# Stacked probability tails for attention, and slot normalisation on other engines, in an attention and soft-MoE kernel

## The reference

```
q = layernorm(x) @ Wq + bq;  k = ctx @ Wk + bk;  v = ctx @ Wv + bv      # 16 heads of 64
p = softmax(where(mask, -1e30, q k^T / 8))                              # 1024 x 154 a head
x = x + (p v) @ Wo + bo
h  = layernorm(x) * norm_g + norm_b
se = (layernorm(slot_embeds) * slot_g + slot_b) * scale                 # 1024 slots x 256
logits = h se^T;  dispatch = softmax over tokens;  combine = softmax over slots
slots = dispatch^T h;  eout = (gelu(slots Wg + bg) * (slots Wu + bu)) Wd + bd
out = x + combine eout
```

## Time and profile before

| | |
|---|---|
| median of 3 runs | 544.62 us (543.82 to 544.94) |
| profiled execution, its own time | 544.24 us |
| its span | 542.5 us, granted TensorE clock 1.00 |
| PE busy | 530.0 us (98%), 3896 matmuls |
| PEld busy | 499.8 us (92%) |
| DVE busy | 434.1 us (80%) |
| ACT busy | 402.2 us (74%) |
| POOL busy | 303.3 us (56%) |

### The profile page before, as it was taken

One profiled execution on the slowest core, in us unless ns is written; L12 is line 12 of the kernel. 1 busy time (PEld: TensorE's weight loads), 2 busy tenths in 40 slices (PEclk: granted clock), 3 DMA queues, 4 the chain that ended last, 5 costly groups with the idle time before them and its releaser, 6 DMA issues.

```text
span 542.5 us, 11967 instructions
## 1 busy us (share of the span) xinstructions
PE 530.0 (98%) x3896; PEld 499.8 (92%) x3896; DVE 434.1 (80%) x1305; ACT 402.2 (74%) x1098; POOL 303.3 (56%) x327
## 2 busy tenths in 40 slices
PE   6999999999999999999998999999999999999997
PEld 4889999999999999999997888999978888899997
DVE  6777878787897979899677998798699888865453
ACT  5879969596896959779564555788979889766562
POOL 6674654544545455454365768787467999910000
DMA  8635000000030000000001333150288888525551
GB/s 257 181 86 179 3 1 2 2 2 1 3 98 2 2 2 1 2 0 4 0 1 80 155 156 156 78 201 1 79 264 283 270 306 288 182 79 170 181 167 67
DMA packets 34901, 54.11 MB, mean 100 GB/s; under 512 B 3997, under 2 KB 21497, under 8 KB 34713
## 3 DMA queue, kind: packets, MB, share of 16 engines
q1 hardware_dynamic: 34841, 53.36, 29.7%
HBM read 40.54 MB, written 10.49 MB: 94 GB/s over the span
## 4 chain that ended last, share of the span: by engine, by line
PE 90%; ACT 4%; DMA 2%; POOL 1%; DVE 1%; issue 1%; SPq 0%; ACTq 0%; DVEq 0%
PE ps L1461 9%; PE ps L1585 9%; PE ps L1357 9%; PE ps L1369 8%; PE ps L1610 8%; PE ps L1499 8%; PE ps L1439 7%; PE ps L1552 7%; PE ps L1476 5%; PE ps L1632 4%; PE ps L1501 4%; PE ps L1644 3%; DMA wvo_raw<-in_L_xattn_Wo_dram 2%; ACT expo L885 1%; PE ps L1615 1%; PE ps L1622 1%
## 5 line engine op out<-in xcount | busy, mean ns | idle before, releaser
L885 ACT ACTIVATE expo<-expo,nmin 128x154 f32<-128x154 f32 x256 | 106.2, 423 | 5.3 <-DVE nmin L1135 4.8
L1135 DVE CUSTOM_DVE_ANT_0 expo<-ps,maskb 128x154 f32<-128x154 f32 x256 | 69.1, 312 | 11.9 <-PE ps L1461 11.9
L723 POOL TENSOR_TENSOR prob_t<-expo,prec 128x104 f32<-128x104 f32 x64 | 23.1, 360 | 89.3 <-DVE prec L1146 89.1
L726 POOL TENSOR_TENSOR prob<-expo,prec 128x512 f32<-128x512 f32 x64 | 66.8, 1043 | 0.0
L1461 PE MATMUL ps<-kbd,qT_high 128*128 128x308 f32 x256 | 61.1, 323 | 0.0
L1155 DVE TENSOR_TENSOR pT_low<-ps,pT_high 128x512 fp32r<-128x512 f32 (+1 forms) x96 | 57.2, 596 | 4.1 <-ACT pT_high L899 3.9
L788 POOL TENSOR_TENSOR w_gu_low<-w_raw,w_gu_high 128x1024 fp32r<-128x1024 f32 x17 | 50.3, 2966 | 16.2 <-ACT w_gu_high L835 16.1
L899 ACT CAST pT_high<-ps 128x512 fp32r<-128x512 f32 (+1 forms) x96 | 49.1, 513 | 10.8 <-PE ps L1476 8.1
L803 ACT ACTIVATE oT_high<-ps,bqv_c 128x256 fp32r<-128x256 f32 x64 | 29.8, 466 | 34.8 <-PE ps L1501 34.7
L885 ACT ACTIVATION_READ_ACCUMULATOR expo<-expo,nmin 128x1 f32 x256 | 50.3, 196 | 0.0
L1461 PEld LDWEIGHTS ps<-kbd,qT_high 128*128 128x128 f32 x256 | 39.8, 190 | 0.2
(11 more groups left out here) (241 smaller groups left out, 1762.7 us busy)
## 6 DMA issues: line engine op xcount, KB each, us to landing
logits_dram<-lsb SPq DMA_DIRECT2D x16, 512.0 KB, 2.6
w_raw<-in_L_ffn_Wg_dram SPq DMA_DIRECT2D x16, 512.0 KB, 4.0
w_raw<-in_L_ffn_Wu_dram SPq DMA_DIRECT2D x16, 512.0 KB, 4.5
w_raw<-in_L_ffn_Wd_dram SPq DMA_DIRECT2D x16, 512.0 KB, 4.5
lraw<-logits_dram SPq DMA_DIRECT2D x13, 512.0 KB, 3.8
out_dram<-gate SPq DMA_DIRECT2D x16, 128.0 KB, 2.2
kbd<-keys SPq DMA_DIRECT2D x12, 154.0 KB, 2.8
wvo_raw<-in_L_xattn_Wv_dram SPq DMA_DIRECT2D x2, 512.0 KB, 7.0
```

Of the source, the lines that this page charges most:

```text
L726: pool.tensor_tensor(prob[:, n % 2, :, heads, :], expo[:, n % 2, pp, :, :, 0:P], prec[:, n % 2, pp].unsqueeze(3).to_broadcast([P, 2, 2, P] ...
L885: ins = act.activation(row, row, ACT.Exp, scale=-1.0, bias=nmin[:, n % 2, pp, j, h:h + 1], accum_out=psums[:, n % 2, pp, j, h:h + 1])
L1135: ins = dve.tensor_tensor_reduce(out=expo[:, n % 2, pp, j, h, :], in0=ps[:, s % NS, h * SK:(h + 1) * SK], in1=maskb[:, (2 * (n // QUADS) + ...
```

## The change

**Tails.** `prob_t` keeps the tails of a pair of heads in 64 columns (52 used, 12 zero), so that `T(n,2)` transposes 128 columns instead of 104. The transposed tails go to `tT_high` and `tT_low`. For each step SP copies them with four DMAs of 64 partitions x 256 columns into `tS`: for a pair, the high half on 64 partitions and the low half on the other 64. The placed value tails `vt` are there twice, on both halves of the partitions. `PV` then does its six main matmuls first, waits for the four DMAs (`d_tt`), and does two tail matmuls (with the high and with the low half of `vt`) instead of three. ACT, before it overwrites `tT`, waits for the DMAs of the step before.

**SP.** Its list becomes one walk over `moves`: key placements, value tails, and from then on each step's four copies. Wo (four pieces), the value tails of the second batch, the second half of x (four pieces), gain and shift, and later the slot embeddings (eight pieces) are asked for three pieces at a time behind a step's copies. `LOADS` changes its order.

**Slot embeddings.** `SB(t)` becomes one ACT operation (scale and bias for each row) and two POOL operations (times `sg_b`, plus `sb_b`) in place of two on DVE; `SA(4)` gets three more short POOL operations.

**Order.** `STEP`, the `EARLY` and `LATER` tables, `PROLOGUE`, `N2_AT` and `YA_AT` are new; `counted` keeps the counts of each engine in order.

```
-STEP = "R1 S00 S01 PV0 T0 LN R0 PV1 Q0 XN S10 Q1 T2 S11 T1 xT0 Y0 xT1 Y1"
+STEP = "R1 S00 S01 Q0 PV0 T2 S10 R0 LN Q1 S11 T0 XN xT0 xT1 PV1 T1 Y0 Y1"
-N2_AT = 19
-YA_AT = {(0, 0): 26, (1, 0): 26, (0, 1): 28, (1, 1): 29}
+N2_AT = 8
+YA_AT = {(0, 0): 25, (1, 0): 28, (0, 1): 33, (1, 1): 30}
+PIECES_A_MOVE = {"K": 0, "VT": 0, "Q": 0, "T": 3}
...
+        def place_tails(ev):
+
+            for half, done in ((0, t_high), (1, t_free)):
+                sp.wait_ge(done, t_no[ev] + 1)
+                for pp in range(2):
+                    to = pp ^ half
+                    sp.dma_start(tS[to * DH:(to + 1) * DH, ev[1] % 2, pp].bitcast(F32), tT[half][pp * DH:(pp + 1) * DH].bitcast(F32))\
+                        .then_inc(d_tt, 16)
...
+            for piece in rest[:PIECES_A_MOVE[ev[0]]]:
+                load_part(*piece)
+            rest = rest[PIECES_A_MOVE[ev[0]]:]
...
+                link(pool.tensor_tensor(srs[:, 1], srs[:, 0], mhalf[:], ALU.pow))
+                link(pool.tensor_tensor(srs[:, 2], smv[:, :, 0], mhalf[:], ALU.mult))
+                link(pool.tensor_tensor(srs[:, 2], srs[:, 2], srs[:, 1], ALU.mult))
+                pool.tensor_tensor(srs[:, 3], srs[:, 2], srs[:, 2], ALU.add).then_inc(se_rstd, 1)
+            elif ev[0] == "SB":
+
+                t = ev[1]
+                if t == 0:
+                    pool.wait_ge(se_scaled, 2)
+                pool.wait_ge(se_norm, t + 1)
+                link(pool.tensor_tensor(se[:, t], se[:, t], sg_b[:], ALU.mult))
+                pool.tensor_tensor(se[:, t], se[:, t], sb_b[:], ALU.add).then_inc(se_ready, 1)
...
+                if t == 2 and n:
+
+                    act.wait_ge(d_tt, 64 * n)
...
+                act.activation(se[:, t], se[:, t], ACT.Identity, bias=srs[:, 3, t:t + 1], scale=srs[:, 1, t:t + 1])\
+                    .then_inc(se_norm, 1)
...
                 for r, (s, m) in enumerate(PASSES):
                     if m == 1:
-                        pe.wait_ge(t_free, both)
+                        pe.wait_ge(t_free, k)
                     for h in range(2):
                         pe.matmul(dst[:, 0:2 * P], vm[s][:, b, p, h * DH:h * DH + P], pT[m][:, n % 2, 2 * pp + h],
                                   start=(r == 0 and h == 0), stop=False)
-                    ins = pe.matmul(dst[:, 0:2 * P], vt[:, b, s, q, pp * P:(pp + 1) * P], pT[m][0:T4, n % 2, 4],
-                                    start=False, stop=(r == 2))
+                pe.wait_ge(d_tt, 64 * (n + 1))
+                for s in range(2):
+                    ins = pe.matmul(dst[:, 0:2 * P], vt[:, b, s, p, :], tS[:, n % 2, pp], start=False, stop=(s == 1))
                 ins.then_inc(acc_full, 1)
```

239 lines of the change are left out of this document (135 added, 104 removed).

## The result

| | median of the runs, us | lowest to highest | profiled execution: own time, span |
|---|---|---|---|
| before | 544.57 (11 runs) | 543.82 to 545.00 | 544.24, 542.5 |
| after | 548.69 (11 runs) | 547.44 to 553.49 | 550.45, 548.6 |

The changed kernel takes 1.0091 times as long, 95% interval 1.0075 to 1.0106: 4.1 us slower, where I forecast 2.4 us faster. Besides the median, look at the spread. Eleven runs of before lie within 1.2 us, those of after within 6.0. Something in the changed kernel differs from one execution to the next.

The account below looks back on a forecast made before the run. The prediction took PE, without slack in attention steps of 6.37 us, to bound the kernel. Its terms summed to -2.4 us, taking the profiled 544.24 to 541.8, so a median of 542.2 us; range 537.0 to 546.4.

Parts of the forecast that it names:

- Tail matmuls, -7.7: Attention's PV: 64 PVs lose one matmul of 0.12 us each, 7.68 us saved; the step becomes 6.14 us.
- Copies, 0 in steady state: Each step's tail copies by SP land before PE needs them, at the median 2.8 us landing: no stall.
- Probabilities, +0.4: Tail transpose early in the next step leaves the probabilities 0.1 us margin; 0.4 us lost over seven steps with xT.
- Start, +1.9: Kernel start: K(3) waits for Wk's second piece, now last in the weights' queue, and starts at 17.5: 1.9 us lost.
- First copies, +0.7: First PV waits for placed value tails and first copies on SP, 9.2 us with 7.7 covered; bounds 0 and 1.5.
- Wo, +0.5: Both Wo splits stand on ACT in one step: 1.3 us lost where 0.8 was; bounds 0 and 2.1.
- Slot statistics and tiles, +2.3 together: Late attention steps: POOL's statistics chain delays step 22's probabilities, 1.3 us; eight slot tiles load ACT further, 1.0 us.
- End, -0.5: End of attention: part of the last Y fills PE's 0.65 us wait for DVE; last copies take 0.2 back.
- The copies late: Rival: slower copy issue makes the last copy 0.3 us late in each of 24 steps, 549.4 us; chance 0.10.
- The probabilities late: Rival: exponential-to-product chain takes 0.15 us more than counted, 24 steps lose up to that, 545.8 us; chance 0.12.
- The slow clock: Rival: PE, idle before 17.5 us, falls back to half clock at the start, 1.5 us more, 543.7 us; chance 0.10.
- All of it holds: Rival: step of 6.14 us, one-off stalls mostly hidden, Wk's piece in time, 537.9 us; chance 0.24.

Follow-up runs that it names:

- e17: Kernel before without one of three tail matmuls per PV (64 fewer), and warming matmuls cut small (66 more): 537.72 us, ratio 0.9874.
- e6: Kernel before with the second of three tail matmuls of each PV left out (64 fewer), nothing else: 542.74 us, ratio 0.9956.
- e4: Changed kernel with the copies of steps 2 to 31, and the waits for them, left out: 543.48 us.
- e9: Changed kernel's tiles, copies, pieces and slot operations in the order of before, tail transpose right behind the first PV: 619.72 us.
- e3: Changed kernel with the second piece of Wk loaded right behind the bias rows instead of last: 548.42 us.
- e5: Changed kernel with 64 matmuls put back, one tail matmul of each PV issued twice: 548.32 us.
- e11: Changed kernel with only the warming matmuls cut small (66 more): 545.15 us, 1.0016 of before.
- e16: Changed kernel with warming matmuls cut small and only the first of eight slot tiles normalised: 543.01 us.
- e18: Changed kernel with warming matmuls cut small and no slot statistics or normalisation during attention: 540.91 us.
- e14: Changed kernel with warming matmuls cut small and POOL's slot-statistics chain put behind the next two probabilities: 545.62 us.
- e1: Changed kernel run again, unedited: 547.25 us.
- e12: Changed kernel with warming matmuls cut small, second Wk piece loaded early and DVE's mask conversion late: 545.44 us.
- e13: The e12 kernel with ACT's cast of Wk's third piece put behind the casts of xT and Wk's second piece: 547.00 us.

## Why the prediction was wrong, step by step

- **Tail matmuls, -7.7.** Right in kind: a PE-bound group fell from 31.71 to 30.77, 0.94 for 8 x 0.12. In the old order 7.0 us arrive at the logits in e17 (281.7 for 288.7) and 5.1 in e6; behind Y(0,0) it is 5.5 in both, where the some 56 of the 64 matmuls that lie there would give 6.7.
- **Copies, 0 in steady state.** Right (e4). They landed in 2.0 us in the median, not 2.8. The Trainium skill's figure of about 2 us ("DMA: Bandwidth & Descriptors", section on latency and other measured facts), which the prediction cited, was the better one.
- **Probabilities, +0.4.** No wait for prob_t in the groups up to 162 us, so nearer 0. How close that chain runs, e9 shows.
- **Start, +1.9.** K(3) came at 17.56 for my 17.5, which is in part luck, since it was not for my reason alone: no wait for wk_low stood there, and the load early (e3) changed nothing. I costed the one load that had moved and did not cost the edits to the orders of DVE and ACT (mask ahead of K(0)'s keys, a 1.06 us cast ahead of xT). A number that comes true does not confirm its mechanism.
- **First copies, +0.7.** 1.07 measured; in the bounds.
- **Wo, +0.5.** The waits are 3.0 us, and taking the splits apart gave 1.4. The failed part is "I take 1.3 us lost where 0.8 was". The first wait, 1.1 us, is ACT's casts and POOL's two subtractions delaying the tail cast. The second, 1.9 us, is the copy behind it: with a packet of PE's code beside it it lands in 3.4 us for 2.0, and with the packet elsewhere the wait is 0.6 us at most (e5, e11 to e16, e18). A code fetch was in no term.
- **Slot statistics and tiles, +2.3 together.** 5.0 us measured for all slot work, at most 4.7 over what before paid. The wait of 1 to 2 us at step 22 came (1.1 us at 209.6). "About 1.4 is covered" and "six of the steps" priced each event by itself; as I read the trace, a lateness of 1 us did not end with its step but ran on through ACT and DVE until the next Y; no run tests that reading, and e14, which took the chain out of that place, moved the loss.
- **End, -0.5.** PE waited 0.9 us for the last copies, not the 0.2 I took. One of them landed in 3.5 us, again with a packet of PE's code beside it (283.9 us), and e1, where it landed in 2.9, has no such wait over 0.5 us.
- **The missing term.** The list had nothing on the experts, since no instruction there changes. It is the larger half: with the packet moved (e11) the changed kernel stands 0.5 us over before, and its own two sets of runs stand 2.1 and 3.5 us over e11, so 2 to 3.5 of the 4.1 us come from the place of the code, in the experts and at the copies. The range ended at 546.4, which holds e11 and not the kernel that ran.
- **The rivals.** The copies late, in each step: no. The probabilities late: only from step 22 on. The slow clock: it did come, in the profile of after in the experts, behind a wait and for 3 us. At the start it came in other profiles (e3, e11, e12, e13, at 21 us and at 63 to 68), but behind the Wo waits or behind DVE and not ahead of K(3), where I put it. All of it holds: no.

## A version that beats both

e17_before_less64_shift: 537.72 us, 0.9874 of before. It is the kernel before, its order untouched, without the product of V's low tail with the high probabilities and with the warming matmuls cut small. It drops one of the three products of a split multiplication for 26 of 154 keys, so the result there is less exact; whoever can't give that up has no faster kernel in this study. The stacked tails keep all products, and in the orders tried here they did not come out ahead (e11 with 0.5 us over before is the nearest).
